# Layer 1 attention of a two-layer transformer kernel: the flags of four heads come from one comparison on VectorE, and ScalarE masks another head of the four

## What is computed

```python
topk = max(1, int(Tx * 0.3))                    # 307 of 1024
scores = jnp.einsum('bhid,bhjd->bhij', q, k) * scale
topk_scores, indices = jax.lax.top_k(scores, topk)
masked = jnp.full_like(scores, -jnp.inf)
masked = masked.at[bi, hi, ti, indices].set(topk_scores)
attn = jax.nn.softmax(masked, axis=-1)
out = jnp.einsum('bhij,bhjd->bhid', attn, v)
```

## Time and profile before

| what | us |
|---|---|
| median of 3 runs (4086.24 to 4089.66) | 4088.49 |
| the profiled execution, its whole time | 4076.11 |
| span of its trace | 4074.2 |
| busy: PE / DVE / ACT / POOL | 2823.3 / 2963.6 / 2477.3 / 1793.1 |
| z (L1348), first to last start | 1294.0 to 3626.8 |
| granted TensorE clock over the span | 0.757 |

### The profile page before, as it was taken

The page is one execution under the profiler, slowest core; times in us unless marked ns, Lnnn a source line. Parts: engine busy times, 40 slices in busy tenths (PEclk is TensorE's granted clock), DMA queues, the critical chain, the costliest instruction groups (busy, mean ns, idle before and its releaser), DMA issues. The chain is left out here.

```text
span 4074.2 us, 92993 instructions
## 1 busy us (share of the span) xinstructions
PE 2823.3 (69%) x25270; PEld 1692.7 (42%) x25318; DVE 2963.6 (73%) x10992; ACT 2477.3 (61%) x4212; POOL 1793.1 (44%) x4286
## 2 busy tenths in 40 slices
PE   3688888849554666656565666666666666665999
PEld 2133333336342444434343444444444444444665
DVE  6677777531454888888787888888888888864444
ACT  2155555624312888867686887888888888862222
POOL 3000000020013777756575776777776767653000
PEclk9699999959765666766666776776776776676999
DMA  3222232100012000001000001000001000000000
GB/s 111 39 36 35 33 39 30 19 8 26 10 50 72 5 4 7 4 4 36 4 4 4 7 4 36 4 7 4 4 13 27 7 4 5 6 1 27 6 8 8
DMA packets 131770, 77.04 MB, mean 19 GB/s; under 512 B 73287, under 2 KB 116055, under 8 KB 131463
## 3 DMA queue, kind: packets, MB, share of 16 engines
q1 hardware_dynamic: 131463, 74.32, 9.5%
HBM read 52.15 MB, written 19.14 MB: 17 GB/s over the span
## 5 line engine op out<-in xcount | busy, mean ns | idle before, releaser
L1130 PE MATMUL a_ST<-a_qs,a_ks 75*128 (+1 forms) x4096 | 732.0, 267 | 555.0 <-ACT a_eT L1174 540.0
L1230 POOL TENSOR_TENSOR a_near<-a_side,a_z 128x1024 int32<-128x1024 int32 x512 | 968.4, 1891 | 47.9 <-POOL a_side L1226 10.3
L1130 PEld LDWEIGHTS a_ST<-a_qs,a_ks 75*128 75x128 bf16 x4096 | 507.2, 125 | 709.8 <-issue 697.0
L1152 ACT ACTIVATE a_signs<-a_z,a_tiny 128x1024 bf16<-128x1024 f32 x512 | 588.3, 1149 | 218.0 <-DVE a_z L1348 203.3
L1348 DVE TENSOR_SCALAR_CACHE_REDUCE a_z<-a_S,a_thr 128x1024 f32<-128x1024 f32 x512 | 650.2, 1270 | 75.8 <-issue 53.8
L1145 ACT ACTIVATE a_signs<-a_S,search 128x1024 bf16<-128x1024 f32 x512 | 569.0, 1111 | 36.4 <-PE a_S L1079 36.4
L706 ACT ACTIVATE a_eT<-a_ST 128x512 f32<-128x512 f32 (+3 forms) x768 | 359.8, 490 | 363.4 <-PE a_ST L659 264.5
L1079 PE MATMUL a_S<-a_ks,a_qs 72*128 72x512 bf16 x1024 | 429.1, 512 | 214.0 <-DVE a_z L1348 163.8
L1174 ACT ACTIVATE a_eT<-a_ST 128x1024 f32<-128x1024 f32 x512 | 518.4, 1013 | 57.8 <-PE a_ST L1131 56.6
L1131 PE MATMUL a_ST<-ident_b,a_mask 128*128 128x128 bf16 x3072 | 505.7, 254 | 0.0
L773 DVE TENSOR_REDUCE a_mx<-a_S 128x1 f32<-128x512 f32 (+3 forms) x768 | 387.8, 535 | 158.2 <-PE a_S L643 110.7
(11 more groups left out here) (331 smaller groups left out, 5837.2 us busy)
## 6 DMA issues: line engine op xcount, KB each, us to landing
a_ks<-k_parts SPq DMA_DIRECT2D x288, 64.0 KB
a_qs<-q_parts SPq DMA_DIRECT2D x144, 64.0 KB
a_qs<-q_parts SPq DMA_DIRECT2D x288, 32.0 KB
a_qs<-a_flip SPq DMA_DIRECT2D x512, 0.8 KB
q_parts<-p_qp SPq DMA_DIRECT2D x48, 128.0 KB, 1.7
k_parts<-p_kp SPq DMA_DIRECT2D x48, 128.0 KB, 1.8
f_w<-L_ffn_W SPq DMA_DIRECT2D x16, 256.0 KB, 2.5
v_ones<-p_vst SPq DMA_DIRECT2D x8, 288.0 KB, 2.4
```

The source lines that it names most:

```text
L1130: pe.matmul(ST[:, block_of], ks[:, hl * SEQ + kb * P:hl * SEQ + (kb + 1) * P], qa, start=True, stop=False)
L1152: act.activation(signs[:, 2, :], z[:, hl % RING, :], ACT.Sign, bias=tiny[:, :], accum_out=sgn[1][:, hl:hl + 1]).then_inc(cnt2, 1)
L1230: pool.tensor_tensor(near[:, hl % 2, :].bitcast(I32), side[:, one].bitcast(I32).broadcast_to([P, SEQ]), z[:, hl % RING, :].bitcast(I32), A ...
```

## The change

- `matched` and `same` go, with POOL's `gap`, ACT's `twice` and `hidden`, and the nop that raised `checked`. In slot 3 DVE writes, for four heads together, 19 columns of signals each: `best == edge` (16), `open_end > edge` (1), `rank` beyond the window (2, both equal). For this `best` has a ring of 8 heads. PE sums 76 columns in one matmul into the same PSUM bank as `OT`; DVE adds up the 19 of each head (`seen`), subtracts 128 (`flags`), both at the end of slot 3, with a wait for each.
- DVE's wait for `flags` stands ahead of z in slot 0. `find_edge` (before: `hits`) comes first in slot 0 and then the first `max` and the read back; the other slots have it after two `max`. In slot 0 DVE makes a mask behind the branch.
- ACT masks the second head of a quad (`ON_ACT = 1`) in slot 1, ahead of its second count; DVE masks heads 0, 2 and 3.
- The transpose of `parts` stands behind z in slot 1, no longer near the slot's end.

```diff
-    MASKS, RING = 4, 8
+    MASKS, RING, ON_ACT = 4, 8, 1
...
-        FL = OT[0:1, 192:196]
+        FL = OT[0:1, P:P + 4 * VIEWS]
...
-                    pe.matmul(FL, k.ones[:, 0:1], twice[:, h0:h0 + 4], start=True, stop=False)
-                    pe.matmul(FL, k.ones[:, 0:1], hidden[:, h0:h0 + 4], start=False, stop=True).then_inc(flag_p, 1)
+                    pe.matmul(FL, k.ones[:, 0:1], signals[:, h0:h0 + 4, :].rearrange("p j c -> p (j c)"), start=True, stop=True).then_inc(flag_p, 1)
...
+                if lagged(it, h, PICK, H, TOTAL) is not None and (h - PICK) % 4 == ON_ACT:
+                    l, hl, q = nth(it, h, PICK), (h - PICK) % H, it * QD + (h - PICK) // 4
+                    act.wait_ge(cut_s, q + 1)
+                    act.wait_ge(mask_s, 3 * q + 1)
+                    if not (isinstance(it, int) and l < MASKS):
+                        act.wait_ge(turned, l - (MASKS - 1))
+                    act.activation(mask[:, hl % MASKS, :], z[:, hl % RING, :], ACT.Relu, bias=cut_steep[:, hl:hl + 1],
+                                   scale=-STEEP).then_inc(mask_a, 1)
                 if lagged(it, h, C2, H, TOTAL) is not None:
                     l, hl = nth(it, h, C2), (h - C2) % H
...
-                    act.wait_ge(same_s, nth(it, h, FLAG) + 1)
-                    act.activation(twice[:, h0:h0 + 4], same[:, h0:h0 + 4], ACT.Square, bias=less1[:, :])
-                    act.wait_ge(gap_s, q + 1)
-                    act.activation(hidden[:, h0:h0 + 4], gap[:, h0:h0 + 4], ACT.Sign).then_inc(bad_s, 1)
-                if lagged(it, h, PICK, H, TOTAL) is not None and (h - PICK) % 4 == 0:
...
-                    pool.tensor_tensor(gap[:, four], open_end[:, four], edge[:, four], ALU.subtract).then_inc(gap_s, 1)
                     pool.wait_ge(cut0_s, q + 1)
-                    pool.tensor_tensor(cut_steep[:, h0:h0 + 1], cut[:, h0:h0 + 1], steep[:, :], ALU.mult).then_inc(cut_s, 1)
+                    pool.tensor_tensor(cut_steep[:, h0 + ON_ACT:h0 + ON_ACT + 1], cut[:, h0 + ON_ACT:h0 + ON_ACT + 1], steep[:, :], ALU.mult).then_inc(cut_s, 1)
...
+                if check:
+                    dve.wait_ge(flag_v, qp + 1)
                 if has1 is not None:
                     dve.wait_ge(thr1_s, l1 + 1)
-                    if h1 % 4 == 0 and not (isinstance(it, int) and l1 < RING):
+                    if h1 % 4 == ON_ACT and not (isinstance(it, int) and l1 < RING):
                         dve.wait_ge(mask_a, it * QD + (h - C2) // 4 - 1)
                     dve.tensor_scalar(z[:, h1 % RING, :], S[h1 % 2][:, :], thr1[:, one1], None, ALU.add, ALU.max,
                                       accum_out=zmax[:, one1]).then_inc(z_s, 1)
@@ -1351,39 +1345,58 @@
                     dve.wait_ge(top_s, l3 + 1)
                 if has2 is not None:
                     dve.wait_ge(near_s, l2 + 1)
-                if check:
-
-                    dve.wait_ge(flag_p, qp + 1)
-                    dve.tensor_scalar(flags[:, :], FL, float(P), None, ALU.add, ALU.add, accum_out=flag_sum[:, :]).then_inc(flag_v, 1)
-                elif picks:
-                    make_mask()
-                if has4 is not None:
+                if lagged(it, h, TOPL, H, TOTAL) is not None and ends(h, TOPL):
+                    q, ring = quad(it, h, TOPL), ((h - TOPL) // 4) % 2
+                    dve.wait_ge(part_s, PART_STEPS * q + PART_STEPS)
+                    if not (isinstance(it, int) and q < 2):
+                        dve.wait_ge(top_in, 16 * 4 * (q - 1))
+                    dve.transpose(flip[:, ring, :], parts[:, ring, :]).then_inc(flip_s, 1)
+
+                def find_edge():
                     dve.wait_ge(rank_s, l4 + 1)
                     dve.wait_ge(sort_s, SORTS * l4 + SORTS)
-                    dve.scalar_tensor_tensor(hits[:, :], odd2[:, :], rank[:, one4], best[:, h4 % 2, :], ALU.is_equal, ALU.mult,
+                    dve.scalar_tensor_tensor(hits[:, :], odd2[:, :], rank[:, one4], best[:, h4 % RING, :], ALU.is_equal, ALU.mult,
                                              accum_out=edge[:, one4]).then_inc(edge_s, 1)
-                if has3 is not None:
-                    dve.max(ranked[:, 0:8], mine).then_inc(sort_s, 1)
-                if has2 is not None:
-                    dve.max(found[:, 0:8], quarter(0))
+
                 if check:
-                    dve.wait_ge(flag_v, qp + 1)
-                if has3 is not None:
-                    dve.wait_ge(sort_s, SORTS * l3 + 1)
-                if has4 is not None:
-                    dve.wait_ge(edge_s, l4 + 1)
-                    dve.tensor_scalar(matched[:, :], best[:, h4 % 2, :], edge[:, one4], None, ALU.is_equal, ALU.add,
-                                      accum_out=same[:, one4]).then_inc(same_s, 1)
-                if check:
+
+                    if has4 is not None:
+                        find_edge()
+                    if has3 is not None:
+                        dve.max(ranked[:, 0:8], mine).then_inc(sort_s, 1)
                     total = dve.value_load(flag_sum[0:1, 0:1].bitcast(I32), min_val=0, max_val=2 ** 31 - 1)
                     with dve.If(total > 0):
                         with dve.Fori(0, 4) as j:
                             general(j, hp, qp)
-                    dve.nop().then_inc(checked, 1)
+                    if has3 is not None:
+                        dve.wait_ge(sort_s, SORTS * l3 + 1)
+                    make_mask()
+                    if has2 is not None:
+                        dve.max(found[:, 0:8], quarter(0))
+                else:
+                    if picks and hp % 4 != ON_ACT:
+                        make_mask()
+                    if has3 is not None:
+                        dve.max(ranked[:, 0:8], mine).then_inc(sort_s, 1)
+                    if has2 is not None:
+                        dve.max(found[:, 0:8], quarter(0))
+                    if has3 is not None:
+                        dve.wait_ge(sort_s, SORTS * l3 + 1)
+                    if has4 is not None:
+                        find_edge()
                 if has3 is not None:
                     dve.match_replace(rest[:, :], ranked[:, 0:8], mine, GONE).then_inc(sort_s, 1)
                 if has2 is not None:
                     dve.max(found[:, 8:16], quarter(1))
+                if has4 is not None and h4 % 4 == 3:
+                    four = slice(h4 - 3, h4 + 1)
+                    wide = lambda a, n: a[:, four].rearrange("p (j o) -> p j o", o=1).broadcast_to([P, 4, n])
+                    views, first_of = signals[:, four, :], (h4 - 3) % RING
+                    dve.tensor_scalar(views[:, :, WINDOW + 1:], wide(rank, 2), float((2 * WINDOW - 1) ** 2) - MISS ** 2, None, ALU.is_gt)
+                    dve.wait_ge(edge_s, l4 + 1)
+                    dve.tensor_tensor(views[:, :, WINDOW:WINDOW + 1], wide(open_end, 1), wide(edge, 1), ALU.is_gt)
+                    dve.tensor_tensor(views[:, :, 0:WINDOW], best[:, first_of:first_of + 4, :], wide(edge, WINDOW),
+                                      ALU.is_equal).then_inc(bad_s, 1)
                 if has2 is not None:
                     dve.max(found[:, 16:24], quarter(2))
                 if has3 is not None:
@@ -1394,12 +1407,9 @@
                     q, h0 = quad(it, h, NL), (h - NL - 3) % H
                     dve.wait_ge(ot, q + 2)
                     dve.reciprocal(rden[:, h0:h0 + 4], OT[:, 0:P].rearrange("p (j c) -> p j c", c=32)[:, :, HD]).then_inc(rd, 1)
-                if lagged(it, h, TOPL, H, TOTAL) is not None and ends(h, TOPL):
-                    q, ring = quad(it, h, TOPL), ((h - TOPL) // 4) % 2
-                    dve.wait_ge(part_s, PART_STEPS * q + PART_STEPS)
-                    if not (isinstance(it, int) and q < 2):
-                        dve.wait_ge(top_in, 16 * 4 * (q - 1))
-                    dve.transpose(flip[:, ring, :], parts[:, ring, :]).then_inc(flip_s, 1)
+                if adds:
+                    dve.wait_ge(flag_p, qc + 1)
+                    dve.tensor_reduce(seen[:, :], FL.rearrange("p (j c) -> p j c", c=VIEWS), AX, ALU.add).then_inc(seen_s, 1)
                 if has2 is not None:
                     dve.max(found[:, 24:32], quarter(3)).then_inc(top_s, 1)
                 if lagged(it, h, NL, H, TOTAL) is not None and ends(h, NL):
@@ -1410,6 +1420,9 @@
                     dve.tensor_tensor(dst, heads[:, :, 0:HD],
                                       rden[:, h0:h0 + 4].rearrange("p (j o) -> p j o", o=1).broadcast_to([P, 4, HD]),
                                       ALU.mult).then_inc(normed, 1)
+                if adds:
+                    dve.wait_ge(seen_s, qc + 1)
+                    dve.tensor_scalar(flags[:, :], seen[:, :], -float(P), None, ALU.add, ALU.add, accum_out=flag_sum[:, :]).then_inc(flag_v, 1)
```

45 lines of the change are left out of this document (19 added, 26 removed).

## The result

| | before | changed |
|---|---|---|
| median us (20 runs each) | 4087.85 | 4099.46 |
| range us | 4075.47 to 4098.42 | 4084.5 to 4106.09 |
| span of the profiled execution, us | 4074.2 | 4089.4 |
| first to last z of layer 1 attention, us | 2332.8 | 2347.7 |

The ratio is 1.0023, interval 1.0013 to 1.0033: slower by about 10 us. The forecast was 4119.5. The sign is right, the size is three times too large, and 4099.46 lies in the range. The stage explains the whole difference of the two spans: 14.9 of 15.2 us.

What follows compares the result with a forecast made beforehand. No engine is held up all the time; DVE is nearest, in chains through POOL's `near` and slot 0's branch. Quads and loop starts +66 us, passes -35, give +31 on the median 4088.49: 4119.5, range 4050 to 4152.

Steps and rivals of the forecast that it cites:

- point 4: Slots 1 and 2: slot 1 loses mask and `matched`, slot 2 waits longer for `near`; -0.72 us a quad, bounds -0.2 and -1.0.
- the loop's start: Quad at a loop's start: the jump comes later, slot 0 gets 0.1 shorter; +0.6 us each for 31, bounds 0 and +1.3.
- The passes: Flag test `open_end > edge`: two of three passes through `general` go, 17.67 us each; -35.3 us, bounds 0 and -53.
- Point 1: Slot 3: edge found after two `max` delays `cut` and `near`; z to end of `near` 5.47 to 5.96, +0.49 us.
- Point 2: DVE in slot 3: 3.90 becomes 4.75 us with two new waits, just level with `near`, so costing nothing more.
- Point 3: Slot 0: mask behind the branch, readback less hidden; end of `near` to next z 3.27 to 3.99, +0.72 us a quad.
- lower bound of +0.4: Slot 0's added time if load and branch overlap `hits` and `max` fully; the upper bound was +0.9.
- A quad: Sum of slot 3, slot 0 and slots 1 and 2: +0.49 + 0.72 - 0.72 = +0.49 us, for 97 quads.
- my bound of 1.4: Loop's start: DVE reaches the jump only when `seen` is there, up to +1.4 us later than before.
- the wait for `seen`: DVE's wait for PE's 76-column sum in slot 3: 0.25 us foreseen; above half a us would prove the forecast wrong.
- The rule of instruction counts: Skill's rule to minimise chained DVE instructions, not semaphores: five go, five come, so DVE even and only the passes count.

Runs made afterwards that it cites:

- edge_first: Changed kernel with `hits` of the fourth head, and the signal of `rank`, ahead of slot 3's two `max`: 4061.16 us, ratio 0.9941 against the kernel before.

## Why the prediction was right in sign and three times too large

- **What bounds the stage.** I called the 31.6 us for `near` the second largest idle time of DVE. That was a misreading: ahead of slot 2's mask there are 55.6 us in 130 waits, and ahead of z, mostly at the jump, 53.8 in 25. Both are in the sum all the same, in point 4 and in the loop's start.
- **The passes.** Right: -35.3 foreseen, 34 to 36 measured in both kernels, and the two at the foreseen places go.
- **Point 1, the edge in slot 3.** Right: 5.96 foreseen, 5.98 measured, and `edge_first` shows that 0.35 of it is the late edge and that this is paid for.
- **Point 2, DVE in slot 3.** 4.75 foreseen, 4.46 measured. PE's sum is there when DVE comes: `seen` begins at 2429.11 without idle. It changes nothing, since `near` sets slot 0 in either case.
- **Point 4, slots 1 and 2.** -0.72 foreseen, -0.77 measured (7.80 on the average). Slot 1 took the foreseen 3.17 at h = 8, and 3.70 at h = 4, where 0.44 of it is the stop ahead of the transpose; slot 2's wait for `near` is shorter there and takes most of that up (7.86 for both slots against 7.77). The wait ahead of slot 2's mask is 0.61 in the quad shown. None of DVE's waits in the stage ends with ACT.
- **Point 3, slot 0, is the term that was mis-sized.** +0.72 foreseen, +0.38 measured (3.35 to 3.73 on the average). Two causes. I took the load-to-next time of the one quad in the rows, 1.29 and 0.1 for the mask's waits, for all; the changed kernel has 1.04 and 1.10 in two of the three quads, since the gap behind the branch there is 0.15 and no longer 0.45, and 1.35 in the third. That is 0.23 less on the average. And the quad in the rows was the shortest of the three: 3.27 to z of slot 1 against 3.35 on the average, 0.08. What came is close to the lower bound of +0.4, but by luck: that bound stood for load and branch overlapping `hits` and `max` fully, and not for a shorter gap. The trace of before couldn't show that the gap depends on the place, because it was 0.44 to 0.48 in all four.
- **A quad** so became 0.13 longer and not 0.49: 0.51 + 0.38 - 0.77 (0.12 with these rounded medians). Of +47.5 us for 97 quads, 12 came. This alone is 35 us too much.
- **The loop's start** was too small: +0.6 foreseen (bounds 0 to 1.3), +1.01 measured, 13 us more than foreseen in all. The jump did come later: z of slot 3 to z of slot 0 went from 5.87 to 7.22, 1.35 more, near my bound of 1.4. But slot 0 got 0.46 longer and not 0.1 shorter: z to z 4.32 before, 4.78 after, with 1.90 from load to mask there, where load to next was 1.25. Slots 1 and 2 lost 0.85, as elsewhere.
- **The new batches** were not in the sum: 8 us. I had named the wait for `seen` as what would prove me wrong if longer than half a us. There are seven such waits, 3.9 on the average, but not for the reason that I looked at (the length of the sum's chain): in PE's queue the sum stood behind scores that wait for a DMA. The three at the end of an iteration are the ones that cost; the others had their like before the change.
- **The sum.** 12 + 31.3 + 8 - 35.3 = +16 instead of +31: the step that failed is point 3's +0.72, which is 33 of the 35 us that the quads were foreseen too long; the loop's start, 13 us too small, and the new batches, 8 us left out, made up 21 of them. The rule of instruction counts that I weighed, by which DVE's side would be even, comes out no better: with the passes equal the change costs 43 to 46 us at an equal count, and reordering alone gave 34 and 52.
- The sum was made on the traced execution and added to the median of three runs. That median, 4088.49, agrees with the 4087.85 of twenty, so no error lies there.

## What to carry to other kernels

Where an engine branches on a value that it loads, put queued work right ahead of the load, enough to last for the load and the branch; what stands behind the branch is bare. Before filling such a gap, look for the wait that lies just beneath it: here a fill of two `max` gave 52 us in one kernel and nothing in the other, where z waited for a buffer that ACT still read. And put small sums that gate the next engine ahead of work that may wait for a DMA in the same queue.
